# Edge tiles of 125 instead of 128 in a graph network on one core

## The chip, the cores and the metric

One core of one Trainium2 chip runs the whole network as one program. The metric is the device time of one execution in microseconds. The kernel before takes 9366.73 us as the median of 3 runs (9366.05 to 9370.35).

## The reference

A graph of N = 6250 nodes with 128 features has E = 200000 edges, sorted by their target node. There is an attention layer and then three layers of message passing, each of which goes over all edges:

```python
# attention layer
xh = (x @ W).reshape(-1, H, C)                      # H = 4 heads of C = 32
alpha = leaky_relu((xh[dst]*a_i).sum(-1) + (xh[src]*a_j).sum(-1), 0.2)
alpha = softmax of alpha over the edges of each dst
x = layernorm(x + segment_sum(xh[src] * alpha, dst))
# three layers of message passing (h is batch-normalised from the second on)
hk  = relu(concat(h[dst], h[src]) @ linA_w.T + linA_b)
w   = sigmoid(hk @ linB_w.T + linB_b)
prop = segment_sum(w * h[src], dst)
h   = relu(concat(h, prop) @ lin_w.T + lin_b)
# end
x = layernorm(x + h @ final_w.T + final_b)
```

## The kernel before, in words

The edges are cut into groups of GE = 512, that is T = 4 tiles of P = 128 edges. Edge p*4 + t of a group lies on partition p in tile t. 200000 edges make 391 groups and a part of one; the list is filled up to NG = 392 groups with edges whose target lies outside every window. Since the targets are sorted, one group touches few neighbouring nodes: its results go into a window of W = 32 nodes that begins at the group's lowest target (a list of further windows exists for groups that need more).

Each of the four passes over the edges is one pipeline over the groups, and the five engines meet only through semaphores:

- GpSimd fetches the rows of the source nodes, 256 floats or 1 KB for each edge. A group takes four indirect DMAs (line 579), one for each tile, of 128 rows each. They go into one of U = 8 buffers of `G`. A gather waits until the buffer is free and until ACT has copied the group's indices into a small tile `idx`; ACT does this four groups ahead (LOOKAHEAD).
- SP loads for each group the offsets of its targets in the window, broadcast over the partitions (`relbc`, from the table `REL` in DRAM), and 32 rows of the target side (`awin` in message passing, `sm` in attention).
- VectorE makes two one-hot matrices: `sel` (edges on partitions, `make_sel`, line 965) and its transpose `selT16` (window nodes on partitions, `make_selT`, line 969). The latter reads `relbc` in order of p and t, and writes bf16 so that each tile's 128 columns lie together: the source is one run of 512, the target 128 steps of p with 4 of t inside, 256 bytes apart.
- TensorE expands the target side to edges (`selT16` times `awin` or `rhs16`), and sums the weighted rows into the window (`G` times `selw` or `R` times `sel`). VectorE adds the hidden layer (line 1341), takes the logits (line 1352), ACT the sigmoid, and VectorE adds the window to `acc`.

Every engine works through its own steps in an order written out by hand (`mp_order`, `gat_order`), with fixed lags between the stages. In the attention layer there are about 25 VectorE operations for each group, in message passing about a dozen.

Before the first pass SP loads the two lists of edges (lines 413 and 414: 97 rows of 2048 numbers, and the remaining 1344 numbers in a row of their own) and behind them all weights. VectorE turns the lists into window bases and offsets, TensorE transposes them into `rel_all` and `idx_all`, and the table of the attention layer is made and stored. ACT loads x with five DMAs of blocks of 125 rows meanwhile. Between the passes come dense stages over the nodes, in blocks of 125.

Of the kernel before, what the change touches and what calls it, by code (L numbers as in the profile page):

```python
# [15 lines left out]
I32 = mybir.dt.int32  # L16
BF16 = mybir.dt.bfloat16
ALU = mybir.AluOpType
ACT = mybir.ActivationFunctionType

P = 128
T = 4
GE = P * T
# [67 lines left out]
def gnn_kernel(nc, x, src, dst, W0, att, linA_w, linA_b, linB_w, linB_b, lin_w, lin_b, gamma, beta, final_w, final_b,  # L91
# [8 lines left out]
    assert NG % U == 0 and QP <= P and L * 4 * D + D <= U * T * 2 * D - N // NB * D  # L100
    QW = GE * CQ
    QF = E // QW
# [20 lines left out]
    with ExitStack() as ctx:  # L123
# [20 lines left out]
        idx_all = sb("idx_all", [P, (NG + LOOKAHEAD) * T], I32)  # L144
        rel_all = sb("rel_all", [P, NG * T])
        idx = sb("idx", [P, U * T], I32)
# [6 lines left out]
        xrel = sb("xrel", [P, T])  # L153
        xidx = sb("xidx", [P, T], I32)
# [7 lines left out]
        ring = sb("ring", [P, 8, GE])  # L162
        relbc = ring[:, 0:4, :]
        selT = ring[:, 4:8, :]
        pen = sb("pen", [P, 2, GE])
        sel = sb("sel", [P, U, T * W])
        selw = sb("selw", [P, 4, T * W])
        selT16 = selT.bitcast(BF16)[:, :, 0:GE]
        awin = sb("awin", [S * W, 4, D], BF16)
        junk = sb("junk", [P, GE])  # L170
        weighted = sb("weighted", [P, 4, T * D])
        R = weighted[:, 0:2, :]
        ex = weighted[:, 2:4, :]
# [5 lines left out]
        e8 = sb("e8", [P, 2, T, 2 * H])  # L179
        den4 = sb("den4", [H, 2, W])  # L180
        al = sb("al", [P, 2, 4, T * H])
# [4 lines left out]
        logit = sb("logit", [P, 4, T])  # L186
        gate = sb("gate", [P, 4, T])
# [222 lines left out]
        def _(sp):  # L410
            sp.wait_ge(pads_filled, 2)
            for tile, lst in ((dstI, dst), (srcI, src)):
                sp.dma_start(tile[0:QF, :], lst[0:QF * QW].rearrange("(q e) -> q e", e=QW)).then_inc(edges_loaded, 16)
                sp.dma_start(tile[QF:QF + 1, 0:E - QF * QW],  # L414
                             lst[QF * QW:E].rearrange("(q e) -> q e", q=1)).then_inc(edges_loaded, 16)

# [56 lines left out]
            def gat_window(k0, off):  # L473
# [3 lines left out]
                sp.dma_start(relbc[:, off % 4, :], REL[bass.ds(k0 + off, 1), :].rearrange("o e -> (o e)")  # L477
# [9 lines left out]
            with extra_windows(sp, 0) as at:  # L487
                sp.wait_ge(x_free, at.w + (at.q + 1))
                sp.sem_inc(waited, 1)
                sp.dma_start(relbc[:, 0, :], REL[bass.ds(at.g, 1), :].rearrange("o e -> (o e)")  # L490
# [14 lines left out]
            with sp.Fori(0, L) as l:  # L505
# [22 lines left out]
                def window(k0, off):  # L528
# [3 lines left out]
                    sp.dma_start(relbc[0:S * W, off % 4, :], REL[bass.ds(k0 + off, 1), :].rearrange("o e -> (o e)")  # L532
# [11 lines left out]
                with extra_windows(sp, l + 1) as at:  # L544
                    sp.wait_ge(x_free, at.w + (at.q + 1))
                    sp.sem_inc(waited, 1)
                    sp.dma_start(relbc[0:S * W, 0, :], REL[bass.ds(at.g, 1), :].rearrange("o e -> (o e)")
# [15 lines left out]
        def _(pool):  # L563
# [8 lines left out]
            def gather(table, width, k0, off, before, freed):  # L572
# [891 lines left out]
        def _(pe):  # L1464
# [40 lines left out]
            def gat_sjT(k0, off, done=gat):  # L1505
# [4 lines left out]
                for t in range(T):  # L1510
                    i = tr(PS[off % 2][:, P * t:P * t + P], Grows[:, off % U, t, D:2 * D], ident[:, :])  # L1511
# [210 lines left out]
```

## Time and profile before

| | |
|---|---|
| median of 3 runs | 9366.73 us |
| span of the profiled execution | 9351.7 us |
| GpSimd busy | 6739.1 us, 72% |
| VectorE busy | 6023.4 us, 64% |
| TensorE busy | 4974.9 us, 53% |
| ACT busy | 1410.9 us, 15% |

The page gives for the profiled execution its span, from the first to the last instruction, and no total of its own; the median of the runs lies 15 us above that span. The share of an engine counts its instructions from start to end. A gather on GpSimd counts for as long as GpSimd makes the list of transfers for it; the rows themselves arrive later, by the DMA engines. What an engine waits for is inferred from the semaphores; "issue" means that nothing in the profile explains the pause.

### The profile page before, as it was taken

The numbers are of one execution on the slowest core, as the hardware profiler recorded it, in microseconds if no ns is written. First come the engines' busy times: TensorE is split into PE (matmuls) and PEld (weight loads), VectorE is DVE, ScalarE is ACT, GpSimd is POOL, SyncE is SP. The second block draws the span as 40 slices with busy tenths as digits, with TensorE's granted clock in tenths as the row PEclk, the third lists the DMA queues.
The fourth block names the chain that finished last, engine by engine and source line by source line (L and its number), as shares of the span: only waits on it lengthen the run. The fifth ranks groups of instructions, "written<-read, shape, count | busy, mean of one in ns | idle before, by whom it ended". The sixth has DMA issues, their size and how long they took to land.

```text
span 9351.7 us, 148690 instructions
## 1 busy us (share of the span) xinstructions
PE 4974.9 (53%) x27078; PEld 4220.6 (45%) x27079; DVE 6023.4 (64%) x26793; ACT 1410.9 (15%) x5406; POOL 6739.1 (72%) x6331
## 2 busy tenths in 40 slices
PE   2777777777744444444454444444445444444445
PEld 1666666666633333333343333333334333333334
DVE  4888888888856555555556555655555555555656
ACT  1222222222410000000020000000002000000002
POOL 1777777777457777777746777777773777777774
PEclk7555555555555555555565555555556555555555
DMA  2444444444344444444434444444443444444443
GB/s 81 138 137 138 138 138 137 137 138 138 92 137 138 138 138 138 138 138 137 138 109 133 139 138 138 139 138 138 138 135 108 139 137 138 139 138 139 138 139 100
DMA packets 752005, 1241.72 MB, mean 133 GB/s; under 512 B 323315, under 2 KB 387641, under 8 KB 751419
## 3 DMA queue, kind: packets, MB, share of 16 engines
q0 software_dynamic: 301056, 822.48, 30.2%
q1 hardware_dynamic: 444380, 413.53, 15.6%
q10 hardware_dynamic: 6275, 3.20, 0.1%
q14 instruction: 283, 2.32, 0.1%
q8 instruction: 11, 0.18, 0.0%
HBM read 1194.48 MB, written 44.13 MB: 132 GB/s over the span
## 4 chain that ended last, share of the span: by engine, by line
POOL 54%; issue 24%; DMA 6%; DVE 5%; PE 5%; SPq 2%; DVEq 1%; POOLq 1%; ACT 0%; ACTq 0%
POOL G L579 54%; DMA G<-mp_rows,idx 3%; DMA G<-gat_rows,idx 2%; PE ps L1646 2%; DVE junk L1352 1%; SPq L520 1%; PE ps L1551 1%; SPq L513 1%; DMA gat_rows<-ring 1%; DMA mp_rows<-acc 0%; PE ps L1511 0%; DVEq L957 0%; SPq L414 0%; DMA mp_dst_rows<-acc 0%; PE ps L1676 0%
## 5 line engine op out<-in xcount | busy, mean ns | idle before, releaser
L579 POOL DMA_INDIRECT G<-mp_rows,idx x4704 | 4920.1, 1046 | 1810.7 <-issue 1391.1
L1646 PE MATMUL ps<-selw,G 128*128 128x32 f32 x9408 | 2222.2, 400 | 468.8 <-DVE selw L1360 462.9
L1646 PEld LDWEIGHTS ps<-selw,G 128*128 128x128 f32 x9408 | 2093.9, 327 | 751.2 <-issue 652.3
L1341 DVE TENSOR_TENSOR pen<-ps,G 128x512 f32<-128x512 f32 x1176 | 813.1, 691 | 2502.2 <-DMA G<-mp_rows,idx 2500.0
L1636 PE MATMUL ps<-awin,ring 96*128 96x128 bf16 x4704 | 714.5, 307 | 2986.2 <-DVE ring L969 2986.2
L969 DVE TENSOR_SCALAR ring<-ring,pF 96x512 bf16<-96x512 f32 (+1 forms) x1568 | 2178.9, 1390 | 2.5 <-DMA sm<-gat_si 2.1
L579 POOL DMA_INDIRECT G<-gat_rows,idx x1568 | 1779.5, 1135 | 552.7 <-issue 526.5
L1636 PEld LDWEIGHTS ps<-awin,ring 96*128 96x128 bf16 x4704 | 404.2, 130 | 3142.9 <-DVE ring L969 3142.9
L1352 DVE SCALAR_TENSOR_TENSOR junk<-pen,cur 128x128 f32<-128x128 f32 x4704 | 1282.3, 328 | 0.1
L787 ACT ACTIVATE gate<-logit,cur 128x4 f32<-128x4 f32 x1176 | 349.6, 297 | 5870.5 <-DVE junk L1352 5263.8
L1551 PE MATMUL ps<-sel,weighted 128*128 128x32 f32 x3136 | 750.7, 404 | 0.0
L1551 PEld LDWEIGHTS ps<-sel,weighted 128*128 128x128 f32 x3136 | 698.0, 327 | 25.3
L1511 PE MATMUL ps<-ident,G 128*128 128x128 f32 x1568 | 428.7, 429 | 345.3 <-DMA G<-gat_rows,idx 344.9
L666 ACT ACTIVATE pen<-ring,negbig 128x512 f32<-128x512 bf16 x392 | 282.9, 722 | 1518.8 <-DVE ring L969 1518.8
L965 DVE TENSOR_TENSOR sel<-iotaF,rel_all 128x128 f32<-128x128 f32 x1568 | 449.6, 287 | 13.0 <-issue 11.6
L996 DVE CUSTOM_DVE_ANT_0 junk<-ps,pen 128x512 f32<-128x512 f32 x392 | 268.7, 685 | 291.0 <-issue 240.9
L1511 PEld LDWEIGHTS ps<-ident,G 128*128 128x128 f32 x1568 | 280.6, 217 | 363.6 <-issue 236.7
L1352 DVE DVE_READ_ACCUMULATOR junk<-pen,cur 128x1 f32 x4704 | 378.8, 81 | 0.0
L1360 DVE TENSOR_TENSOR selw<-sel,gate 128x128 f32<-128x128 f32 x1176 | 334.6, 285 | 0.2
L654 ACT COPY idx<-idx_all 128x4 int32 (+1 forms) x1572 | 284.3, 182 | 40.7 <-issue 40.6
L1105 DVE TENSOR_TENSOR weighted<-G,weighted 128x512 f32<-128x512 f32 x392 | 270.9, 691 | 0.0
L1523 PE MATMUL ps<-rhs,ring 128*128 128x24 bf16 x1568 | 106.6, 184 | 281.4 <-DVE rhs L1035 281.3
(176 smaller groups left out, 5146.1 us busy)
## 6 DMA issues: line engine op xcount, KB each, us to landing
ring<-rel_dst SPq DMA_DIRECT2D x1176, 192.0 KB
ring<-rel_dst SPq DMA_DIRECT2D x392, 256.0 KB
G<-mp_rows,idx POOLq DMA_INDIRECT x4704
awin<-mp_dst_rows SPq DMA_DIRECT2D x1176, 24.0 KB
G<-gat_rows,idx POOLq DMA_INDIRECT x1568
mp_rows<-acc SPq DMA_DIRECT2D x30, 625.0 KB
mp_dst_rows<-acc SPq DMA_DIRECT2D x30, 468.8 KB
sm<-gat_si SPq DMA_DIRECT2D x392, 0.5 KB
```

The lines of the kernel that those rows point to most:

```text
L579: pool.indirect_dma_start(out=G[:, u, width * t:width * (t + 1)], out_offset=None, in_=table, in_offset=bass.IndirectOffsetOnAxis(ap=idx[: ...
L654: nc.scalar.copy(idx[:, T * (off % U):T * (off % U) + T], idx_all[:, bass.ds(k0 * T + off * T, T)]).then_inc(idx_ready, 1)
L787: nc.scalar.activation(gate[:, off % 4, :], logit[:, off % 4, :], ACT.Sigmoid, bias=cur[:, C_BB:C_BB + 1]).then_inc(done["gate"], 1)
L965: v.tensor_tensor(sel[:, off % U, :].rearrange("p (t n) -> p t n", t=T), iotaW, rel4, ALU.is_equal).then_inc(made, 1)
L969: v.tensor_scalar(tile[0:rows, off % 4, :].rearrange("n (t p) -> n p t", t=T), relbc[0:rows, off % 4, :].rearrange("n (p t) -> n p t", t=T ...
L1341: v.tensor_tensor(pen[:, off % 2, :].rearrange("p (t c) -> p t c", t=T), PS[off % 2][:, :].rearrange("p (t c) -> p t c", t=T), Grows[:, of ...
L1352: v.scalar_tensor_tensor(junk[:, P * t:P * t + P], pen[:, off % 2, P * t:P * t + P], 0.0, cur[:, C_B:C_B + D], ALU.max, ALU.mult, accum_ou ...
L1360: v.tensor_tensor(selw[:, off % 4, :].rearrange("p (t n) -> p t n", t=T), sel[:, off % U, :].rearrange("p (t n) -> p t n", t=T), gate[:, o ...
L1511: i = tr(PS[off % 2][:, P * t:P * t + P], Grows[:, off % U, t, D:2 * D], ident[:, :])
L1551: i = mm(PS[4 + b][:, 0:W], R[:, b, D * t:D * t + D], sel[:, off % U, W * t:W * t + W], start=(t == 0), stop=(t == T - 1))
L1636: i = mm(PS[off % 2][:, D * t:D * t + D], selT16[0:S * W, off % 4, P * t:P * t + P], awin[:, off % 4, :], start=True, stop=True)
L1646: i = mm(PS[2 + off % 2][:, 0:W], Grows[:, off % U, t, 0:D], selw[:, off % 4, W * t:W * t + W], start=(t == 0), stop=(t == T - 1))
```

## The change

A tile has EP = 125 edges, so a group has GE = 500, and 200000 edges are exactly NG = 400 groups on QP = 100 rows of 2000 numbers. No edge is filled in. All tensors with edges on partitions have 125 of them; each gather has 125 rows; `selT16` keeps its buffer but uses 500 of its columns, 125 for each tile. Each list is loaded with one DMA. Everything else stays: the window of 32, the 8 buffers, the orders and lags.

```diff
-GE = P * T
+EP = 125
+GE = EP * T
...
-    QF = E // QW
...
-        idx = sb("idx", [P, U * T], I32)
+        idx = sb("idx", [EP, U * T], I32)
...
-        ring = sb("ring", [P, 8, GE])
+        ring = sb("ring", [P, 8, P * T])
+        Gedge = Grows[0:EP]
...
             for tile, lst in ((dstI, dst), (srcI, src)):
-                sp.dma_start(tile[0:QF, :], lst[0:QF * QW].rearrange("(q e) -> q e", e=QW)).then_inc(edges_loaded, 16)
-                sp.dma_start(tile[QF:QF + 1, 0:E - QF * QW],
-                             lst[QF * QW:E].rearrange("(q e) -> q e", q=1)).then_inc(edges_loaded, 16)
+                sp.dma_start(tile, lst.rearrange("(q e) -> q e", e=QW)).then_inc(edges_loaded, 16)
...
                     pool.indirect_dma_start(
-                        out=G[:, u, width * t:width * (t + 1)], out_offset=None, in_=table,
+                        out=G[0:EP, u, width * t:width * (t + 1)], out_offset=None, in_=table,
                         in_offset=bass.IndirectOffsetOnAxis(ap=idx[:, T * u + t:T * u + t + 1], axis=0),
                     ).then_inc(gathered[u], 16)
...
             def make_selT(k0, off, tile, rows, node, made):
                 v.tensor_scalar(tile[0:rows, off % 4, :].rearrange("n (t p) -> n p t", t=T),
-                                relbc[0:rows, off % 4, :].rearrange("n (p t) -> n p t", t=T),
+                                relbc[0:rows, off % 4, 0:GE].rearrange("n (p t) -> n p t", t=T),
                                 node, None, ALU.is_equal).then_inc(made, 1)
...
-                        i = mm(PS[off % 2][:, D * t:D * t + D], selT16[0:S * W, off % 4, P * t:P * t + P],
+                        i = mm(PS[off % 2][0:EP, D * t:D * t + D], selT16[0:S * W, off % 4, EP * t:EP * t + EP],
                                awin[:, off % 4, :], start=True, stop=True)
```

## Rows read from the trace of the kernel before

**Rows 1.** The page: span, and busy time of each engine (share of the span).
```profile
span 9351.7 us, 148690 instructions
PE 4974.9 (53%) x27078; PEld 4220.6 (45%) x27079; DVE 6023.4 (64%) x26793; ACT 1410.9 (15%) x5406; POOL 6739.1 (72%) x6331
```

**Rows 2.** The chain that ended last: shares by engine; SPq is SP's queue.
```profile
POOL 54%; issue 24%; DMA 6%; DVE 5%; PE 5%; SPq 2%; DVEq 1%; POOLq 1%; ACT 0%; ACTq 0%
```

**Rows 3.** Line 579, GpSimd's gathers: duration min/median/max; idle before them.
```profile
L579 POOL DMA_INDIRECT G<-mp_rows,idx x4704: 942/947/1943, 2605.0 to 9267.3; - x196
L579 POOL DMA_INDIRECT G<-gat_rows,idx x1568: 942/948/1979, 196.5 to 2452.5; - x196
  issue: 1917.7, 6048
  ACT idx L654: 154.8, 155
```

**Rows 4.** The page's groups for the gathers: busy us, mean ns of one.
```profile
L579 POOL DMA_INDIRECT G<-mp_rows,idx x4704 | 4920.1, 1046 | 1810.7 <-issue 1391.1
L579 POOL DMA_INDIRECT G<-gat_rows,idx x1568 | 1779.5, 1135 | 552.7 <-issue 526.5
```

**Rows 5.** Waits: who waited for whom; us in total, times, longest.
```profile
DVE pen L1341 <- DMA G<-mp_rows,idx: 2500.0, 1143, 3.9
```

**Rows 6.** Timelines, GpSimd and VectorE: start us, duration us, what.
```profile
4000.87 1.36 DVE L969 TENSOR_SCALAR ring<-ring,pF 96x512 bf16<-96x512 f32 x1
4001.09 1.45 POOL L579 DMA_INDIRECT G<-mp_rows,idx  x1 [0.30 <-issue]
4002.84 0.95 POOL L579 DMA_INDIRECT G<-mp_rows,idx  x1 [0.30 <-issue]
...
1205.57 1.72 POOL L579 DMA_INDIRECT G<-gat_rows,idx  x1 [0.30 <-issue]
1205.79 1.38 DVE L969 TENSOR_SCALAR ring<-ring,pF 128x512 bf16<-128x512 f32 x1
```

**Rows 7.** Line 969 on VectorE: duration min/median/max in ns.
```profile
L969 DVE TENSOR_SCALAR ring<-ring,pF x1568: 1347/1357/1604, 203.7 to 9265.5; 96x512 bf16<-96x512 f32 x147, 128x512 bf16<-128x512 f32 x49
```

**Rows 8.** Two windows: us, then busy us (instructions) of PE, PEld, DVE, ACT, POOL.
```profile
300.00:2300.00 2000.00, 1469.68 (x10077) 1256.50 (x10078) 1629.59 (x8707) 582.86 (x1740) 1577.37 (x1388) 0.50 0.49 138
2700.00:4500.00 1800.00, 832.86 (x4002) 708.57 (x4002) 1071.71 (x4332) 131.27 (x666) 1394.80 (x1331) 0.50 0.48 138
```

**Rows 9.** VectorE operations that show its pace: duration, or group mean.
```profile
L879 DVE CAST acc<-acc x1: 1227/1227/1227, 76.5 to 76.5; 98x2048 f32<-98x2048 int32 x1
L881 DVE TENSOR_REDUCE moreF<-acc x1: 2286/2286/2286, 77.7 to 77.7; 98x4 f32<-98x2048 f32 x1
L1299 DVE TENSOR_SCALAR ring<-mh x150: 210/221/440, 2573.0 to 7148.4; 128x125 f32 x90, 128x125 f32<-128x125 f32 x60
L893 DVE COPY rel_all<-ps x4: 818/826/843, 90.5 to 93.1; 128x392 f32<-128x392 f32 x4
L929 DVE TENSOR_SCALAR ring<-ps 125x128 f32<-125x128 f32 x50 | 14.5, 291 | 33.3 <-DMA gat_rows<-ring 31.3 <-PE ps L1500 1.8
```

**Rows 10.** The start: SP's issue of a list, and the two waits.
```profile
5.62 11.05 SPq L414 DMA_DIRECT2D acc<-in_dst  x1
17.38 30.66 SPq L414 DMA_DIRECT2D acc<-in_src  x1
DVE acc L879 <- DMA acc<-in_src: 66.4, 1, 66.4
PE ps L1468 <- DMA params<-in_L_gnn_lin_b: 86.6, 1, 86.6
```

**Rows 11.** DMA queues (packets, MB, share of 16 engines); one issue.
```profile
q0 software_dynamic: 301056, 822.48, 30.2%
q10 hardware_dynamic: 6275, 3.20, 0.1%
G<-in_x ACTq DMA_DIRECT2D x5, 625.0 KB
```

More of the change, by code:

```diff
@@ L99, in gnn_kernel @@
     NG = QP * CQ
-    assert NG % U == 0 and QP <= P and L * 4 * D + D <= U * T * 2 * D - N // NB * D
     QW = GE * CQ
-    QF = E // QW
+    assert NG % U == 0 and QP <= P and QW * QP == E and L * 4 * D + D <= U * T * 2 * D - N // NB * D
     NT = N // (NB * BU)
@@ L142, in gnn_kernel @@
         relF = mh[0:QP, 0:QW]
-        idx_all = sb("idx_all", [P, (NG + LOOKAHEAD) * T], I32)
-        rel_all = sb("rel_all", [P, NG * T])
-        idx = sb("idx", [P, U * T], I32)
+        idx_all = sb("idx_all", [EP, (NG + LOOKAHEAD) * T], I32)
+        rel_all = sb("rel_all", [EP, NG * T])
+        idx = sb("idx", [EP, U * T], I32)
         per_group = sb("per_group", [P, NG], I32)
@@ L152, in gnn_kernel @@
         shift = sb("shift", [P, 1])
-        xrel = sb("xrel", [P, T])
-        xidx = sb("xidx", [P, T], I32)
+        xrel = sb("xrel", [EP, T])
+        xidx = sb("xidx", [EP, T], I32)
         baseF = sb("baseF", [P, CQ])
@@ L161, in gnn_kernel @@
         Grows = G[:, :, :].rearrange("p u (t c) -> p u t c", t=T)
-        ring = sb("ring", [P, 8, GE])
+        ring = sb("ring", [P, 8, P * T])
+        Gedge = Grows[0:EP]
         relbc = ring[:, 0:4, :]
         selT = ring[:, 4:8, :]
-        pen = sb("pen", [P, 2, GE])
-        sel = sb("sel", [P, U, T * W])
-        selw = sb("selw", [P, 4, T * W])
+        pen = sb("pen", [P, 2, P * T])
+        sel = sb("sel", [EP, U, T * W])
+        selw = sb("selw", [EP, 4, T * W])
         selT16 = selT.bitcast(BF16)[:, :, 0:GE]
         awin = sb("awin", [S * W, 4, D], BF16)
-        junk = sb("junk", [P, GE])
+        junk = sb("junk", [P, P * T])
         weighted = sb("weighted", [P, 4, T * D])
-        R = weighted[:, 0:2, :]
-        ex = weighted[:, 2:4, :]
+        R = weighted[0:EP, 0:2, :]
+        ex = weighted[0:EP, 2:4, :]
         mx = sb("mx", [P, 4, 2])
@@ L178, in gnn_kernel @@
         dg = sb("dg", [P, 2, S, W], BF16)
-        e8 = sb("e8", [P, 2, T, 2 * H])
+        e8 = sb("e8", [EP, 2, T, 2 * H])
         den4 = sb("den4", [H, 2, W])
-        al = sb("al", [P, 2, 4, T * H])
+        al = sb("al", [EP, 2, 4, T * H])
         mnew = sb("mnew", [P, 2, W])
@@ L185, in gnn_kernel @@
         tt = sb("tt", [P, 2, 2, 2 * W])
-        logit = sb("logit", [P, 4, T])
-        gate = sb("gate", [P, 4, T])
+        logit = sb("logit", [EP, 4, T])
+        gate = sb("gate", [EP, 4, T])
         flat = ring[:, :, :].rearrange("p a b -> p (a b)")
@@ L588, in gather_extra @@
                     pool.indirect_dma_start(
-                        out=G[:, 0, TW * t:TW * (t + 1)], out_offset=None, in_=table,
+                        out=G[0:EP, 0, TW * t:TW * (t + 1)], out_offset=None, in_=table,
                         in_offset=bass.IndirectOffsetOnAxis(ap=xidx[:, t:t + 1], axis=0)).then_inc(x_rows, 16)
@@ L665, in gat_pen @@
                 act.wait_ge(done["selT"], k0 + (off + 1))
-                nc.scalar.activation(pen[:, off % 2, :], selT16[:, off % 4, :], ACT.Identity, bias=negbig[:, 0:1],
+                nc.scalar.activation(pen[:, off % 2, 0:GE], selT16[:, off % 4, :], ACT.Identity, bias=negbig[:, 0:1],
                                      scale=BIG).then_inc(done["pen"], 1)
@@ L876, in _ @@
             assert done[0] == PREP_CONST
-            dve.wait_ge(edges_loaded, 64)
+            dve.wait_ge(edges_loaded, 32)
             then(v.tensor_copy(dstF, dstI))
@@ L1162, in make_extra_sel @@
                 v.tensor_scalar(tile[0:rows, 0, :].rearrange("n (t p) -> n p t", t=T),
-                                relbc[0:rows, 0, :].rearrange("n (p t) -> n p t", t=T),
+                                relbc[0:rows, 0, 0:GE].rearrange("n (p t) -> n p t", t=T),
                                 shift[0:rows, 0:1], node, ALU.subtract, ALU.is_equal).then_inc(selT_done, 1)
```

50 lines of the change are left out of this document (25 added, 25 removed).

## The prediction

> **What bounds the kernel now.** I read the busy times first, then the chain of waits, then the groups of the gather line, and last short timelines. The busy times [rows 1] put GpSimd first at 72% of the span, and the chain [rows 2] names its gathers for 54% and "issue" for 24%. The reader is to see in the gather line [rows 3] that nearly all idle time before a gather has nobody behind it: 1917.7 us over 6048 gathers is 0.30 us each, while ACT's index copies account for 154.8 us. So GpSimd issues one gather, pauses 0.30 us, issues the next, and the others follow: VectorE stands 2500.0 us in the message passing waiting for rows [rows 5]. An undisturbed gather takes 0.947 us. Four of them with their pauses are 4 x (0.947 + 0.30) = 4.99 us a group. That is the floor of a group. The actual group is longer: in the two windows [rows 8] there are 1388/4 = 347 groups in 2000 us (5.76 us each, attention layer) and 1331/4 = 333 groups in 1800 us (5.41 us each, message passing).
>
> Where is the rest? The mean gather is 1046 and 1135 ns [rows 4], against medians of 947 and 948 ns [rows 3]. The excess is 4920.1 - 4704 x 0.947 = 465 us and 1779.5 - 1568 x 0.948 = 293 us, together **758 us**. The timelines [rows 6] say what it is. The gather that starts at 4001.09 lasts 1.45 us and the next one 0.95; VectorE's L969 (the transposed one-hot, 512 elements) runs from 4000.87 to 4002.23, and the gather ends 0.31 us behind it. In the attention layer the gather at 1205.57 lasts 1.72 us, L969 ends at 1207.17 and the gather 0.12 us later. A gather cannot finish while L969 runs. L969 is 1.357 us long by its median [rows 7] and there is one in each group.
>
> **The change part by part.** (a) *More groups.* 392 become 400 in each of four passes, so 6400 gathers for 6272: 128 x 1.247 = 160 us more, if a gather of 125 rows costs what one of 128 does. Bounds for a gather: in proportion to rows 0.925 us (-142 us over 6400); the other end is the first rival. I take 0.947, because no row shows a smaller one and the start and end of an instruction do not shrink with rows.
>
> (b) *L969.* Its source is one run of 512 values, its target 128 rows of 4 (p outside, t inside). Afterwards: one run of 500, and 125 rows of 4. What makes it stop GpSimd? Copies in SBUF run two elements at a time here: the cast of 2048 values takes 1227 ns and the reduction of as many 2286 ns [rows 9]. I read this as the instruction taking a second path to memory, splitting its data in halves, and GpSimd needing that same path. Line 1299, 125 elements of SBUF on both sides, takes 221 ns by its median; line 929, the same kind of operation on 128 elements out of PSUM, 291 ns [rows 9]. The 70 ns between them are what 125 elements cost less at 0.60 in place of 1.12 ns each (65 ns). So an odd count is no obstacle when both sides have it. With 500 on one side and 125 on the other the halves no longer correspond: 500 halves at 250, which is row 62 and a half of 125. I expect it to fall back to one element at a time on one path, and GpSimd not to be stopped. By the Trainium skill, page "VectorE: DVE Perf Modes", section "Mode 2×_2P", this mode needs an outermost non-unit dimension that is even, or odd and equal on both sides; 500 against 125 is neither. The page "SBUF — State Buffer", section "Who interferes with whom", has the same mode and GpSimd exclude one another; by that, the trace agrees, with ends 0.12 and 0.31 us behind L969.
>
> Of the 758 us I take 90%, 680 us, as removed; the rest I leave to short casts and to operations with two inputs in SBUF, which stay.
>
> How long L969 then is, no row shows. Low end: 500 elements at the reduction's pace of 2286/2048 = 1.12 ns, 0.56 us. High end: now 256 steps of two in 1.357 us; 500 steps of equal length are 2.65 us. Nearest is line 893 [rows 9], which writes single elements with gaps: 392 in 826 ns, 2.1 ns each, so 1.05 us. I take 1.05 to 1.36, no longer than now. Its cover: VectorE is busy 1629.59/347 = 4.70 us a group in the attention layer and 1071.71/333 = 3.22 us in the message passing [rows 8], under 4.99 in both. At 2.65 us it would be 5.99 and 4.51: the attention layer would go over.
>
> (c) *Loading the edge list.* Each list was loaded as 97 rows of 8 KB and a rest. SP stands 30.66 us in issuing the second [rows 10], before it 11.05 us for the first; all weights queue behind, TensorE waits 86.6 us for the last of them and VectorE 66.40 us for the list, and that is on the chain of the start. Now it is one load of 100 rows each. A load of 125-row blocks by ACT is 6250 packets of rows and 25 more, 5 for each of 5 DMAs [rows 11]: five engines share it, five being what divides 125 and is at most 16. 97 is prime, so one engine does all 97; 100 would go on ten. The 42 us of issue fall to a few: **-40 us**, with bounds of 0 and -43, once.
>
> (d) *Everything else* (125 partitions in place of 128, 500 in place of 512 columns in ACT's and VectorE's instructions, the two memsets and the transposes of 125 columns) is on engines that wait for GpSimd. At most 12/512 of an instruction. I set 0. Without the cover, in the attention layer, VectorE's slack is 4.99 - 4.70 = 0.29 us a group, and its loads would still fit. The lists of indices are copied four groups ahead, some 20 us, so that a gather landing a microsecond later delays only the end of a pass.
>
> Sum against the profiled execution: 9351.7 - 680 + 160 - 40 = 8792 us of span. The median of the runs is 9366.7, 15 us above the span. So 8807, rounded **8810 us**, 5.9% below before.
>
> **Rivals.** *First, the other side: 125 rows go on five engines, and building the list for them is slower.* [Rows 11] show it for the ACT queue. The gathers now make 301056/6272 = 48 packets, 3 for each of 16 engines, so 8 rows per engine; five engines would have 25 rows each. If GpSimd writes for all engines side by side, the part that writes grows by 25/8. That part is what a gather still does once L969 lets go, 0.12 to 0.31 us: +0.25 to +0.66 us a gather, times 6400 = +1600 to +4200 us, giving 10410 to 13000 us. It decides from +0.087 us a gather (557/6400). For it: the packets of ACT's loads, and the shape of GpSimd's work as the stall shows it. Against: GpSimd's DMAs need not be shared out as ACT's are, and the engine's work may be per row. The skill's page "DMA: Bandwidth & Descriptors", section "Why a DMA increments its semaphore by 16 and not by 1", says that the largest number up to 16 that divides both row counts is taken, and grants the software-generated direct copies an exception. It speaks against this change. With it alone and a flat price per gather the sum would stay 8810, since consecutive gathers start on different engines.
>
> *Second: L969 stays in the two-path mode.* Then (b) gives nothing and 32 more groups bring 32 x 758/1568 = 15 us of stall: 9367 + 160 + 15 - 40 = 9500 us. For it: L969 takes 1.357 us, hardly a two-at-a-time speed, so that its mode is read only from whom it stops.
>
> *Third: L969 doubles (2.65 us).* Message passing is unharmed, attention becomes VectorE's at 5.99 us: 8810 + 400 x 1.0 = 9210 us.
>
> *Fourth: the gather gets cheaper with its rows*, 8810 - 142 = 8670, or a little under.
>
> **How the numbers follow.** Forecast 0.50, first rival 0.28, second 0.10, third 0.08, fourth 0.04. The forecast's own range is 8700 to 8950. The whole range must go from the fourth case to the lower end of the first rival: 8640 to 10400 leaves out some 0.03 below and half of the first rival above, 0.14. A change under 0.2% could not be told from none here. Faster: 0.50 + 0.08 + 0.04 less 0.02 = 0.60; slower 0.37; the same 0.03, mostly a first rival that costs just what the stalls give.
>
> **What would show it.** In the profile after: gathers with mean near median, 0.95 to 0.97 us, also where L969 lies beside them (b); a group of 5.0 to 5.1 us in both windows; 6400 gathers; the wait for `in_src` and TensorE's first wait some 40 us shorter, and the first gather before 160 us in place of 196.5 (c). A median gather above 1.03 us makes the forecast wrong, and then the packets per gather (48 now) say whether five engines carry it. Stalls as now beside L969 mean the second rival; VectorE without idle time in the attention layer the third.

## The result and the profile after

The changed kernel takes 10731.9 us as the median of 4 runs (10726.06 to 10734.05), beside 9368.54 us (9366.05 to 9372.19, 4 runs) for the kernel before: a ratio of 1.1455, interval 1.1439 to 1.1471. It is 14.6% slower. The forecast was 8810 us, with a range up to 10400. In one set of the runs below, e1 to e3, which ran on another chip than the later ones (15, they on 4), the kernel before took 10917.72 us (10876.9 to 10972.25, 7 runs) in place of some 9363, for a reason that no trace here shows; ratios of that set are beside that number, and what rests on them was run again.

The page of the kernel after: the span, the busy time of each engine, then the chain that ended last.

```profile
span 10732.3 us, 151490 instructions
PE 5282.3 (49%) x27598; PEld 4610.9 (43%) x27599; DVE 7883.0 (73%) x27305; ACT 1423.2 (13%) x5494; POOL 7887.8 (73%) x6459
...
POOL 48%; issue 28%; DVE 10%; PE 5%; DMA 4%; DVEq 2%; SPq 2%; POOLq 1%; ACT 0%; ACTq 0%
```

Two engines have grown against [rows 1]: GpSimd by 1149 us and VectorE by 1860 us. The chain has the same two leaders as in [rows 2], and VectorE at twice its share. Which instructions grew is in the views by line. Below are the gathers (now line 578) and the transposed one-hot (now line 968): duration min/median/max in ns, first and last start.

```profile
L578 POOL DMA_INDIRECT G<-mp_rows,idx x4800: 1207/1214/1558, 3007.9 to 10647.7; - x192
L578 POOL DMA_INDIRECT G<-gat_rows,idx x1600: 1207/1214/1728, 142.3 to 2839.0; - x178
...
L968 DVE TENSOR_SCALAR ring<-ring,pF x1600: 2408/2414/2431, 150.1 to 10646.6; 96x500 bf16<-96x500 f32 x133, 128x500 bf16<-128x500 f32 x45
```

Beside [rows 3] and [rows 7], the shortest gather went from 942 to 1207 ns and the median from 947 to 1214: a gather is 0.267 us longer. Line 968 went from 1357 to 2414 ns. The longest message passing gather fell from 1943 to 1558 ns, and the page's means show the same:

```profile
L578 POOL DMA_INDIRECT G<-mp_rows,idx x4800 | 5875.7, 1224 | 1832.9 <-issue 1711.9
L578 POOL DMA_INDIRECT G<-gat_rows,idx x1600 | 1972.6, 1233 | 802.1 <-issue 506.1
```

Mean over median is 10 and 19 ns here, where [rows 3, 4] have 99 and 187. A timeline of GpSimd and of VectorE says why (start, duration, what):

```profile
4000.35 1.21 POOL L578 DMA_INDIRECT G<-mp_rows,idx  x1 [0.30 <-issue]
4001.86 1.21 POOL L578 DMA_INDIRECT G<-mp_rows,idx  x1 [0.30 <-issue]
...
3999.40 2.41 DVE L968 TENSOR_SCALAR ring<-ring,pF 96x500 bf16<-96x500 f32 x1
...
4004.61 0.69 DVE L1340 TENSOR_TENSOR pen<-ps,G 125x512 f32<-125x512 f32 x1 [1.58 <-DMA G<-mp_rows,idx]
```

The gather at 4000.35 starts and ends (4001.56) inside line 968, which runs to 4001.81, and takes its usual 1.21 us. In [rows 6] both gathers beside that line ended only behind it. The queue of the gathers (packets, MB, share of 16 engines) has changed too:

```profile
q0 software_dynamic: 819200, 826.65, 30.3%
```

That is 819200/6400 = 128 packets for each gather, against 48 in [rows 11], for fewer rows. The records of the packets in the trace have their sizes: of the data, 30 packets of 4096 bytes (4 rows) and 5 of 1024 bytes (1 row) for each gather, where the kernel before has 32 of 4096. Five engines with 25 rows each make just that, 5 x (6 x 4 + 1) rows; sixteen engines with 8 rows each, the last with 5, would make 31 and 1. What the other packets are, the run of sizes below shows.

Where the time went, by windows (us, then busy us and instructions of PE, PEld, DVE, ACT, POOL, then granted clock, busy share of the DMA engines and GB/s), one in the attention layer and one in message passing:

```profile
300.00:2200.00 1900.00, 1258.17 (x8072) 1089.04 (x8071) 1618.41 (x6968) 459.22 (x1395) 1381.23 (x1121) 0.50 0.46 114
3400.00:4400.00 1000.00, 420.94 (x1960) 372.46 (x1961) 703.33 (x2130) 64.60 (x328) 800.66 (x655) 0.50 0.48 120
```

With four gathers a group these are 280 and 164 groups: **6.78** us a group in attention and **6.11** in message passing, where [rows 8] give 5.76 and 5.41. In message passing 4 x (1.222 + 0.305) = 6.11: GpSimd alone sets it. In attention that floor would be 6.15 and the group is 0.6 us above it. Over the passes: 400 x 6.78 - 392 x 5.76 = +454 us, 1200 x 6.11 - 1176 x 5.41 = +970 us, and the first gather starts at 142.3 us in place of 196.5 [rows 3], -54 us. The sum is +1370 of the 1380.6 us by which the span grew.

### The profile page after: what moved, and what is told of

Read it like the earlier page. It is cut to its first block, busy times and chain, and to the rows that moved or that the text cites. A ratio compares the mean times of both kernels' runs of the same rounds, so it can differ in the third digit from the quotient of the medians.

```text
span 10732.3 us, 151490 instructions
## 1 busy us (share of the span) xinstructions
PE 5282.3 (49%) x27598; PEld 4610.9 (43%) x27599; DVE 7883.0 (73%) x27305; ACT 1423.2 (13%) x5494; POOL 7887.8 (73%) x6459
## 3 DMA queue, kind: packets, MB, share of 16 engines
q0 software_dynamic: 819200, 826.65, 30.3%
## 4 chain that ended last, share of the span: by engine, by line
POOL 48%; issue 28%; DVE 10%; PE 5%; DMA 4%; DVEq 2%; SPq 2%; POOLq 1%; ACT 0%; ACTq 0%
POOL G L578 48%; DMA G<-mp_rows,idx 3%; PE ps L1522 2%; DVE sm L1006 1%; DVE junk L1351 1%; SPq L512 1%; DVE sel L964 1%; SPq L519 1%; DVE rhs L1034 1%; PE ps L1550 1%; DVEq L956 1%; DMA gat_rows<-ring 1%; DVE weighted L1104 0%; DVE sm L1012 0%; DVE mh L1097 0%
## 5 line engine op out<-in xcount | busy, mean ns | idle before, releaser
L578 POOL DMA_INDIRECT G<-mp_rows,idx x4800 | 5875.7, 1224 | 1832.9 <-issue 1711.9
L968 DVE TENSOR_SCALAR ring<-ring,pF 96x500 bf16<-96x500 f32 (+1 forms) x1600 | 3863.2, 2415 | 2.5 <-DMA sm<-gat_si 2.1
L1635 PE MATMUL ps<-awin,ring 96*125 96x128 bf16 x4800 | 826.2, 327 | 3821.8 <-DVE ring L968 3821.8
L1645 PE MATMUL ps<-selw,G 125*128 125x32 f32 x9600 | 2267.6, 400 | 448.3 <-DVE selw L1359 448.3
L1645 PEld LDWEIGHTS ps<-selw,G 125*128 125x128 f32 x9600 | 2136.7, 328 | 642.1 <-issue 560.3
L1340 DVE TENSOR_TENSOR pen<-ps,G 125x512 f32<-125x512 f32 x1200 | 829.5, 691 | 2104.8 <-DMA G<-mp_rows,idx 2102.9
L1635 PEld LDWEIGHTS ps<-awin,ring 96*125 96x125 bf16 x4800 | 601.4, 218 | 3984.1 <-DVE ring L968 3984.1
L1351 DVE SCALAR_TENSOR_TENSOR junk<-pen,cur 125x128 f32<-125x128 f32 x4800 | 1375.5, 339 | 0.1
L1550 PE MATMUL ps<-sel,weighted 125*128 125x32 f32 x3200 | 766.1, 404 | 0.0
L1550 PEld LDWEIGHTS ps<-sel,weighted 125*128 125x128 f32 x3200 | 712.2, 327 | 25.8
```

The lines of the kernel that those rows point to most:

```text
L578: pool.indirect_dma_start(out=G[0:EP, u, width * t:width * (t + 1)], out_offset=None, in_=table, in_offset=bass.IndirectOffsetOnAxis(ap=id ...
L968: v.tensor_scalar(tile[0:rows, off % 4, :].rearrange("n (t p) -> n p t", t=T), relbc[0:rows, off % 4, 0:GE].rearrange("n (p t) -> n p t", ...
L1340: v.tensor_tensor(pen[0:EP, off % 2, :].rearrange("p (t c) -> p t c", t=T), PS[off % 2][0:EP, :].rearrange("p (t c) -> p t c", t=T), Gedge ...
L1351: v.scalar_tensor_tensor(junk[0:EP, P * t:P * t + P], pen[0:EP, off % 2, P * t:P * t + P], 0.0, cur[0:EP, C_B:C_B + D], ALU.max, ALU.mult, ...
L1550: i = mm(PS[4 + b][:, 0:W], R[:, b, D * t:D * t + D], sel[:, off % U, W * t:W * t + W], start=(t == 0), stop=(t == T - 1))
L1635: i = mm(PS[off % 2][0:EP, D * t:D * t + D], selT16[0:S * W, off % 4, EP * t:EP * t + EP], awin[:, off % 4, :], start=True, stop=True)
```

## The experiments

Three causes stand to be told apart, all of them in the prediction: the 125-row gather is dearer because five engines carry it (first rival); line 968 has lost the two-path mode, which frees GpSimd (the forecast) but doubles the line (third rival); the edge lists load faster. Each can be done or undone alone. Kernels of one set ran on one chip beside the kernel before.

**The kernel after again (e5).** Nothing was changed.

> The kernel after, unchanged, beside the kernel before in the same stretch of chip time. In the last group of runs the kernel before took 10918 us instead of 9369 with the same program, and gathers whose list took 0.949 us were waited for longer. Theory C (that stretch had slower landings of rows, which a kernel of 16-engine gathers at 1.25 us each feels and one of 1.5 us each hardly does): where the kernel before is again near 10900, the kernel after is near 10750 to 10950, that is no slower; where the kernel before is near 9370, the kernel after is 10730. Rival D (everything is slower by a factor): the ratio stays at 1.145.

Measured: 10712.89 us (10708.24 to 10721.68), ratio 1.1443 (1.1424 to 1.1462) beside 9363.19 us. The result repeats, and the numbers below are held against this one.

**Only the 125-row gather, put into the kernel before (e8).** The groups stay 512 edges in tiles of 128; from the ninth group of each pass a gather fetches 125 rows, so that the last three edges of a tile work on old rows. The same edit from the first group on (e4) gives no time, since those edges then have no rows at all.

```diff
+                def rows(n, t):
+                    return dict(out=G[0:n, u, width * t:width * (t + 1)], out_offset=None, in_=table,
+                                in_offset=bass.IndirectOffsetOnAxis(ap=idx[0:n, T * u + t:T * u + t + 1], axis=0))
+                if isinstance(k0, int):
+                    for t in range(T):
+                        pool.indirect_dma_start(**rows(P, t)).then_inc(gathered[u], 16)
+                else:
+                    for t in range(T):
+                        pool.indirect_dma_start(**rows(125, t)).then_inc(gathered[u], 16)
```

> The kernel before, with only the gathers changed to 125 rows after the first eight groups of each pass; the last three edges of a tile keep older rows, so part of the work is left out. L969 with both paths stays. Theory A: undisturbed gathers 1.214 us, 128 packets each; message passing 6.1 to 6.5 us a group and attention 6.1 to 6.8 us, 9367 + about 1500 us = 10700 to 11100 us where the kernel before is near 9370. Rival B (the shape of the gather costs nothing, groups of 500 do): the time of the kernel before.

Measured: 10641.56 us (10639.77 to 10650.6), ratio 1.1366 (1.1347 to 1.1385). Its gathers and the one-hot, then the two windows (the same columns as above):

```profile
L586 POOL DMA_INDIRECT G<-mp_rows,idx x4608: 1180/1201/2202, 2978.1 to 10554.7; - x192
L583 POOL DMA_INDIRECT G<-mp_rows,idx x96 | 92.5, 964 | 299.0 <-DMA mp_rows<-acc 270.6
...
300.00:2200.00 1900.00, 1228.20 (x8427) 1053.89 (x8427) 1410.17 (x7259) 505.05 (x1452) 1545.86 (x1163) 0.50 0.46 120
3400.00:4400.00 1000.00, 400.07 (x1924) 340.43 (x1924) 524.40 (x2080) 63.12 (x320) 804.94 (x641) 0.50 0.45 118
```

Line 583 has the gathers of 128 rows in the same execution, 964 ns in the mean and 949 by the median; line 586 those of 125, 1201 ns by the median. Three rows fewer cost 0.25 us more. The windows have 1900/(1163/4) = 6.53 us a group in attention and 1000/(641/4) = 6.24 in message passing. This one edit makes 1278 us of slowdown, nearly as much as the whole change (the expectation's lowest time was 10700). The stalls are still there (up to 2202 ns), since the one-hot was left alone.

**Only the gathers taken back to 128 rows in the kernel after (e1, e9).** Tiles stay 125 edges; three rows that nobody reads are fetched with each. The index tiles get 128 partitions and are zeroed once.

```diff
-        idx_all = sb("idx_all", [EP, (NG + LOOKAHEAD) * T], I32)
+        idx_all = sb("idx_all", [P, (NG + LOOKAHEAD) * T], I32)
...
-        idx = sb("idx", [EP, U * T], I32)
+        idx = sb("idx", [P, U * T], I32)
...
-                        out=G[0:EP, u, width * t:width * (t + 1)], ...
+                        out=G[:, u, width * t:width * (t + 1)], ...
```

> The kernel after, with each gather of 128 rows instead of 125: the three extra partitions of every tile fetch row 0 and nobody reads them. Groups stay at 500 edges, so L968 stays as it is. Theory A (a gather costs what its most loaded engine has rows: 25 now, 8 then): the gather falls from 1.214 to 0.947 us, a message-passing group from 6.08 to about 5.0 us, the three passes by 3 x 400 x 1.07 = 1280 us; the attention pass, which waits for VectorE, stays near 6.7 us a group or loses up to 0.3. Time 9350 to 9450 us. Theory B (the price lies in the groups of 500, in the longer L968 or in the DMA traffic, not in the shape of the gather): gathers stay near 1.2 us and the time above 10500.

Measured in the first set (e1): 11363.97 us, ratio 1.0406 (1.0365 to 1.0447), beside an expected 9350 to 9450. The gather's median is 0.949 us, as expected, but the time says little: VectorE waited 2024.9 us before line 1343, which adds the rows of message passing, and the profile names nothing on this core for it. So it was run again.

> The same kernel as e1 (after, with gathers of 128 rows of which three are unread; L968 unchanged, 2.41 us on one path), hoped for beside a kernel before near 9363 us. Gathers 0.947 us. Theory A: the message passing is bound by GpSimd again, 4.99 to 5.1 us a group instead of 6.1, so 3 x 400 x 1.05 = 1260 us less than the kernel after; the attention pass is bound by VectorE and its exchange with TensorE and stays at 6.5 to 6.7 us a group. Time 9400 to 9450 us. Rival (VectorE with 2.41 us binds message passing as well once gathers are short): 9700 us or more. Beside a slow kernel before (near 10900) it is near 11360 again.

Measured (e9): 9429.16 us (9423.8 to 9430.03), ratio 1.0071 (1.0055 to 1.0086) beside 9361.9 us. Its gathers, the one-hot, its queue and the windows:

```profile
L579 POOL DMA_INDIRECT G<-mp_rows,idx x4800: 941/949/1064, 2918.9 to 9338.3; - x192
L579 POOL DMA_INDIRECT G<-mp_rows,idx x4800 | 4635.3, 966 | 1852.5 <-issue 1447.2
L579 POOL DMA_INDIRECT G<-gat_rows,idx x1600 | 1535.5, 960 | 1145.4 <-ACT idx L654 591.4
L971 DVE TENSOR_SCALAR ring<-ring,pF x1600: 2407/2414/2436, 152.7 to 9336.7; 96x500 bf16<-96x500 f32 x133, 128x500 bf16<-128x500 f32 x45
...
q0 software_dynamic: 307200, 839.27, 30.9%
...
300.00:2200.00 1900.00, 1302.70 (x8359) 1127.78 (x8358) 1660.84 (x7203) 474.09 (x1440) 1107.87 (x1155) 0.50 0.44 119
3400.00:4400.00 1000.00, 507.99 (x2364) 449.70 (x2364) 842.66 (x2562) 77.80 (x394) 760.21 (x787) 0.50 0.53 146
```

307200/6400 is 48 packets again, and 1284 us are gone. This is the forecast's kernel with its assumption about the gather made true, so its windows test the rest. Message passing: 787/4 = 197 groups, **5.08** us each, as forecast (5.0 to 5.1). Attention: 1155/4 = 289 groups, **6.58** us, where the forecast had about 5.05. GpSimd is busy 58% of that window and VectorE 87%: there VectorE sets the pace, and e7 below shows that it is the one-hot.

**A one-hot without the two-path mode, in the kernel before (e3, e10).** The same elements in the same order, but as an operation on two tensors, the node number broadcast as the second one.

```diff
-                v.tensor_scalar(tile[0:rows, off % 4, :].rearrange("n (t p) -> n p t", t=T),
+                v.tensor_tensor(tile[0:rows, off % 4, :].rearrange("n (t p) -> n p t", t=T),
                                 relbc[0:rows, off % 4, :].rearrange("n (p t) -> n p t", t=T),
-                                node, None, ALU.is_equal).then_inc(made, 1)
+                                node.unsqueeze(2).to_broadcast([rows, P, T]), ALU.is_equal).then_inc(made, 1)
```

> The kernel before, with L969 as a comparison of two tensors (the node numbers broadcast as second tensor) in the same order of elements, so that it cannot use both paths; 128 rows and 512 edges stay. Theory A (one element at a time, each step as long as a step of two before): L969 takes 512/500 x 2.41 = 2.47 us and stops no gather: message passing 4 x 1.25 = 5.0 us a group instead of 5.41 (-480 us), attention 6.6 to 6.7 us a group instead of 5.76 (+350 us): about 9240 us. Rival (the longer L968 in the kernel after came from the odd pitch of 125, not from the lost path): L969 stays near 1.36 us or shorter and the time is about 8700 us.

> The same kernel as e3: the kernel before with L969 as a comparison of two tensors in the old order. It showed 2.42 us for L969, twice as long, and gathers of 1.30 us in the mean that were stopped all the same (longest 2.7 us), so a second tensor read from SBUF stops GpSimd too. Expected beside a kernel before near 9363: message passing 4 x (1.30 + 0.31) = 6.4 us a group, attention 6.7 to 7.0: about 11000 us. Rival (the length came from the slow stretch of that job): L969 1.36 us and no change of time.

Measured: in the first set (e3) 11510.68 us, ratio 1.0539 (1.0504 to 1.0573); run again (e10) 10827.92 us (10820.53 to 10830.5), ratio 1.1562 (1.1544 to 1.1579). The gathers and the one-hot of e10, and a piece of its timeline:

```profile
L579 POOL DMA_INDIRECT G<-mp_rows,idx x4704: 942/946/2712, 2860.9 to 10742.9; - x196
L969 DVE TENSOR_TENSOR ring<-ring,pF x1568: 2417/2421/2493, 204.3 to 10741.6; 96x512 bf16<-96x512 f32 x147, 128x512 bf16<-128x512 f32 x49
...
4003.60 0.95 POOL L579 DMA_INDIRECT G<-mp_rows,idx  x1 [0.31 <-issue]
4004.85 2.17 POOL L579 DMA_INDIRECT G<-mp_rows,idx  x1 [0.30 <-issue]
...
4004.27 2.42 DVE L969 TENSOR_TENSOR ring<-ring,pF 96x512 bf16<-96x512 f32 x1
```

The length is the same as in the kernel after, 2421 for 2414 ns: one element at a time, each step 4.7 to 4.8 ns. But the gather beside it is held, from 4004.85 to 4007.02, and ends 0.33 us behind line 969 (4006.69). An operation with two inputs in SBUF stops GpSimd as well, for nearly twice as long as the two-path one did, and e3's expectation that no gather would be held is false. So e10 shows the length of a single-path step, not what freeing GpSimd brings. The Trainium skill, page "SBUF — State Buffer", section "Who interferes with whom", says both that an operation with two SBUF inputs contends with GpSimd's reads and, as an inference, that descriptor generation is not held by it; here the gather is held, with a longest of 2712 ns against a median of 946. A gather also reads its row numbers from `idx` in SBUF, so the first statement may be enough for this; the run doesn't tell the two apart.

**A one-hot that is one plain run (e2, e6, e7).** Edge t*128 + p of a group goes to partition p of tile t (t*125 + p in the kernel after). Then source and target of the one-hot are both one run, with no hops.

```diff
-                v.tensor_scalar(tile[0:rows, off % 4, :].rearrange("n (t p) -> n p t", t=T),
-                                relbc[0:rows, off % 4, :].rearrange("n (p t) -> n p t", t=T),
+                v.tensor_scalar(tile[0:rows, off % 4, :],
+                                relbc[0:rows, off % 4, :],
                                 node, None, ALU.is_equal).then_inc(made, 1)
...
-                               lst[:, GE * c:GE * c + GE].rearrange("q (p t) -> q p t", t=T)[:, :, t],
+                               lst[:, GE * c:GE * c + GE].rearrange("q (t p) -> q p t", t=T)[:, :, t],
```

On the kernel after with its 125-row gathers (e2), in the first set:

> The kernel after, with edge t*125 + p of a group in tile t instead of edge p*4 + t, so that L968 reads and writes one run of 500 on both sides. Gathers stay at 125 rows. Theory A (VectorE's long L968 binds only the attention pass; the message passing is bound by gathers of 1.214 us): L968 falls from 2.41 to about 0.42 us, the attention group from 6.74 to about 6.1 us, message passing stays at 6.1: 10732 - 400 x 0.65 = about 10470 us. Since 500 on both sides splits evenly, the instruction stops GpSimd again, but only for 0.4 us. Rival (L968 costs in all four passes): below 10000 us.

Measured: 10546.56 us, ratio 0.9657 (0.9624 to 0.969). Line 968 has a median of 472 ns, the gathers one of 1211. GpSimd's longer gathers set its pace: both passes stay near 4 x (1.23 to 1.27 + 0.305) us a group. Since the kernel after was not run in that set, this run doesn't say what the plain run is worth to it. On the kernel before (e6), and on the kernel after with 128-row gathers (e7):

> The kernel before with edge t*128 + p in tile t, so that L969 is one run of 512 on both sides, 128 rows for each gather. Theory A (GpSimd's stalls are the length of L969 with both paths): L969 0.42 to 0.53 us, GpSimd stopped at most half as often and long, message passing 5.0 to 5.15 us a group and attention 5.0 to 5.2: where the kernel before takes 9370, about 8800 us. Rival (the stalls have another cause and only coincide with L969): no change. Where rows land slowly (the kernel before near 10900) the gain may be smaller.

> The kernel after with both costs removed: gathers of 128 rows (three of them unread) and L968 as one run of 500. Theory A (the 400 groups by themselves cost only 2% more gathers): e6 plus 128 x 1.25 us = 160 us, less 54 us for the shorter start, about 1.012 times e6. Rival (groups of 500 or tiles of 125 have a cost of their own on TensorE or VectorE): more than 1.03 times e6.

Measured, beside 9363.19 us: e6 8854.34 us (8848.54 to 8865.79), ratio 0.9458 (0.9442 to 0.9473); e7 8869.33 us (8868.43 to 8875.11), ratio 0.9471 (0.9455 to 0.9486). The one-hot and the gathers of e6, then the attention window of e7:

```profile
L969 DVE TENSOR_SCALAR ring<-ring,pF x1568: 470/477/731, 206.6 to 8763.8; 96x512 bf16<-96x512 f32 x147, 128x512 bf16<-128x512 f32 x49
L579 POOL DMA_INDIRECT G<-mp_rows,idx x4704: 942/946/1407, 2391.9 to 8764.3; - x196
...
300.00:2200.00 1900.00, 1593.10 (x10447) 1396.71 (x10447) 1455.02 (x9006) 600.56 (x1803) 1460.83 (x1442) 0.50 0.56 149
```

512 elements take 477 ns instead of 1357, 0.93 ns each against the 1.12 of an operation that goes one at a time [rows 9], so still in the two-path mode, and gathers are still held (the longest takes 1407 ns), but for a third as long at most. e7 against e9 isolates the form of the one-hot in the kernel with tiles of 125: its line has a median of 471 ns, 9429 - 8869 = 560 us are gone, and the attention window goes from 6.58 to 1900/(1442/4) = 5.27 us a group. e7 had been put some 1.2% above e6 for its 128 additional gathers; it is 0.2% above. The earlier lists were in that sum already (first gather at 143.7 instead of 198.9 us); what was not is that its gathers are held less: above 0.947 or 0.946 us each, the gathers lose 187 us in e7 and 268 in e6. Why they are held less, no run shows.

**Gathers of other sizes (e11).** In the kernel before, from the ninth group on, odd groups gather 128, 120, 126 and 124 rows, even ones 112, 64, 100 and 127. Rows not fetched are left out of the work.

```diff
+                    if off % 2:
+                        pool.indirect_dma_start(**rows(128, 0)).then_inc(gathered[u], 16)
+                        pool.indirect_dma_start(**rows(120, 1)).then_inc(gathered[u], 16)
+                        pool.indirect_dma_start(**rows(126, 2)).then_inc(gathered[u], 16)
+                        pool.indirect_dma_start(**rows(124, 3)).then_inc(gathered[u], 16)
...
```

> The kernel before with gathers of different sizes after the first eight groups of each pass, each on a line of its own (part of the work is left out): 128, 120, 126 and 124 rows in the odd groups, 112, 64, 100 and 127 in the even ones. Theory A (length = 0.82 us + 15.7 ns for each row of the most loaded engine, where the number of engines is the largest up to 16 that divides the rows; from 8 rows in 0.947 us and 25 in 1.214): 128 0.95, 120 (15 engines, 8 rows) 0.95, 126 (14, 9) 0.96, 124 (4, 31) 1.31, 112 (7 rows) 0.93, 64 (4) 0.88, 100 (10 engines, 10 rows) 0.98, 127 (1 engine, 127) 2.8 us. Rival (only full 16 have a fast path, everything else the price of 125): 120, 126, 100 near 1.2 us as well.

Measured once (10899.9 us): lines 586 to 589 are 128, 120, 126 and 124 rows, 591 to 594 are 112, 64, 100 and 127.

```profile
L586 POOL DMA_INDIRECT G<-mp_rows,idx x576: 1132/1205/1648, 3007.3 to 10807.2; - x192
L587 POOL DMA_INDIRECT G<-mp_rows,idx x576: 986/993/1100, 3008.8 to 10808.7; - x192
L588 POOL DMA_INDIRECT G<-mp_rows,idx x576: 995/999/1371, 3010.1 to 10810.0; - x192
L589 POOL DMA_INDIRECT G<-mp_rows,idx x576: 1292/1297/1309, 3011.7 to 10811.3; - x192
L591 POOL DMA_INDIRECT G<-mp_rows,idx x576: 940/944/1433, 2999.5 to 10799.7; - x192
L592 POOL DMA_INDIRECT G<-mp_rows,idx x576: 912/916/942, 3001.3 to 10801.0; - x192
L593 POOL DMA_INDIRECT G<-mp_rows,idx x576: 1002/1007/1989, 3002.5 to 10802.2; - x192
L594 POOL DMA_INDIRECT G<-mp_rows,idx x576: 2565/2982/3581, 3004.5 to 10804.3; - x192
```

Take the number of engines as the largest divisor of the rows up to 16, and look at the rows that each then has. 64: 4 rows, 916 ns. 112: 7 rows, 944. 128: 8 rows, 947 (in its own kernel). 120 on 15: 8 rows, 993. 126 on 14: 9 rows, 999. 100 on 10: 10 rows, 1007. 125 on 5: 25 rows, 1214 (in the kernel after). 124 on 4: 31 rows, 1297. 127 on 1: 127 rows, 2565 at the least. The duration goes with this number and not with the rows: 124 rows cost more than 125, and 127 far more than either. Between 8 and 25 rows an engine's row costs 15.7 ns, from 31 to 127 about 13 ns by the least duration.

The packets settle it. Past the first eight groups each size is gathered 768 times. By this rule, with up to 4 rows in a packet, the eight sizes together make 201 packets of 4096 bytes, 21 of 3072, 10 of 2048 and 14 of 1024; the trace has 154368, 16128, 7680 and 10752, which is 768 times these numbers. All other packets are of 4, 8, 12 and 16 bytes, and their numbers (99840, 4608, 20736 and 435456) are 768 times what comes out when each gather ends with one of 4 bytes on all 16 engines and an engine that carries no row gets 4 bytes in place of each row that a carrying engine has. In the kernel after that makes 16 x 8 = 128 packets a gather. So GpSimd's list has 16 entries for each row of an engine, 16 x 25 = 400 for 125 rows and 16 x 8 = 128 for 128 rows. The trace doesn't name the engine of a packet; that the idle ones get these fillers follows from the numbers, which agree for every size. That only counts divisible by 16 are cheap, the rival in that expectation, is false: 120, 126 and 100 cost 40 to 60 ns over 128, no more. A 128-row gather right behind the 127-row one takes 1205 ns; why was not pursued, and the order of the sizes was not varied, so a part of the 40 to 60 ns can come from what stands before them.

**The version that beats both (e12).** The kernel before with the plain-run one-hot of e6, and with its lists loaded as 96 rows, one row and the rest.

```diff
-                sp.dma_start(tile[0:QF, :], lst[0:QF * QW].rearrange("(q e) -> q e", e=QW)).then_inc(edges_loaded, 16)
+                sp.dma_start(tile[0:QF - 1, :],
+                             lst[0:(QF - 1) * QW].rearrange("(q e) -> q e", e=QW)).then_inc(edges_loaded, 16)
+                sp.dma_start(tile[QF - 1:QF, :],
+                             lst[(QF - 1) * QW:QF * QW].rearrange("(q e) -> q e", q=1)).then_inc(edges_loaded, 16)
```

> e6 (before, L969 as one run of 512) with each list of edges loaded as 96 rows, one row and the rest instead of 97 rows and the rest. Theory A (96 rows go over 16 engines, 97 over one): the weights come 40 us earlier, the first gather at about 145 us instead of 199, and the time is 40 to 54 us below e6: about 8805 us where the kernel before takes 9363. Rival (the start is bound by the loads of x and the table): below e6 by less than 10 us.

Measured: 8812.0 us (8799.69 to 8815.53, 5 runs), ratio 0.9407 (0.9394 to 0.9419), 42 us below e6. Its first gather starts at 139.7 us, 59 us before that of e6. SP's issues of the first list and the start of the second (start, duration):

```profile
5.22 0.40 SPq L413 DMA_DIRECT2D acc<-in_dst  x1
5.68 0.31 SPq L415 DMA_DIRECT2D acc<-in_dst  x1
6.04 0.23 SPq L417 DMA_DIRECT2D acc<-in_dst  x1
6.31 0.33 SPq L413 DMA_DIRECT2D acc<-in_src  x1
```

The rows of the kernel before [rows 10] need care: line 414, where SP stood 11.05 and 30.66 us, is the list's last, single row of 1344 numbers, not the load of 97 rows, which line 413 issued in 0.35 and 0.62 us. In e12 the same single row (line 417) is issued in 0.23 us. So it isn't dear by itself; SP stands at the next issue behind a load of 97 rows, and behind one of 96 it doesn't.

## Why the prediction was wrong

**Step (a), more groups: this failed.** It priced a gather of 125 rows at 0.947 us, "because no row shows a smaller one", though its bounds ran up to the first rival. Measured is 1.214 us, because five engines carry 25 rows each and the list grows with the rows of one engine. Over 6400 gathers that is 6400 x 0.267 = 1709 us of GpSimd's time; the time itself moves by 1278 us (e8) or 1284 us (e9 against e5), since a part falls where GpSimd was held or was not the bound: in attention e9 has 6.58 us a group and the kernel after only 6.78. The first rival had the mechanism (five engines), the place of decision (+0.087 us a gather) and a price of +0.25 to +0.66 us that holds the measured 0.267 at its low end (its premise that GpSimd writes for all engines side by side is what the packets show; the 0.12 us at which it put the part that grows was read from a single gather), and its lowest time, 10410, is 3% under what came. It got 0.28 and should have been the forecast. (200000 edges of 512 a group are 390 groups and a part of one, not the 391 of the description; the sums go by the 392 that are gathered, and stay.)

Its grounds against were weak. The prediction had the packets of ACT's 125-row loads [rows 11] and the 48 packets of a gather, 3 for each of 16 engines, which is what the same rule gives for 128. The Trainium skill, page "DMA: Bandwidth & Descriptors", section "Why a DMA increments its semaphore by 16 and not by 1", excepts some software-generated direct copies; a gather is indirect, and its packets follow the rule. With the rule and the flat price the prediction would have kept 8810; what the forecast left out, and its rival had, was that GpSimd's list grows with the rows of one engine.

**Step (b), line 969 leaves the two-path mode: right, and GpSimd is no longer stopped.** In e9 the means are 966 and 960 ns with medians of 949 and 947 (forecast 0.95 to 0.97 us), and message passing has its 5.08 us a group. By that half 680 us were to go; the 758 us over the medians in the kernel before are 4635.3 - 4800 x 0.949 = 80 us and 1535.5 - 1600 x 0.947 = 20 us in e9, so 658 us of stall went. That the unequal odd count is what ends the mode is the prediction's reading; no run varies the count. The prediction's pause of 0.30 us between gathers was rounded down (1917.7/6048 is 0.317), which leaves its 4.99 us a group a little under the 5.08.

**The length of that line failed too.** It was set at 1.05 to 1.36 us, "no longer than now"; it is 2.414 us. The nearest row taken, line 893, is a different operation out of PSUM. The working had the right answer as its high end: 500 steps of the present length, 2.65 us. A two-path step took 1357/256 = 5.3 ns, a single-path step 2414/500 = 4.8 ns, so losing the mode nearly doubles the line. The third rival (0.08) said exactly this, with attention at 5.99 us a group and 9210 us. Measured in e9: 6.58 and 9429. What it missed is a pause. Below are VectorE's wait at line 998 of e9 (us in total, times, longest) and three starts of that line, which runs once in each group:

```profile
DVE junk L998 <- issue: 256.8, 50, 5.5
...
301.96 0.68 DVE L998 CUSTOM_DVE_ANT_0 junk<-ps,pen 128x500 f32<-128x500 f32 x1 [5.29 <-issue]
...
307.59 0.67 DVE L998 CUSTOM_DVE_ANT_0 junk<-ps,pen 128x500 f32<-128x500 f32 x1
...
313.52 0.67 DVE L998 CUSTOM_DVE_ANT_0 junk<-ps,pen 128x500 f32<-128x500 f32 x1
```

A group without a pause is 313.52 - 307.59 = 5.93 us, the rival's 5.99. But 50 times in 400 groups, once in each turn of the loop of eight, VectorE pauses for 5.1 us (256.8/50); an eighth of that is 0.64 us a group, and 5.93 + 0.64 = 6.57 against 6.58 in the window. The kernel before has the pause as well (240.9 us in 44 pauses before line 996), but there GpSimd has only its 0.30 us between two gathers, (2000 - 1577.37)/1388 [rows 8], so GpSimd sets the pace and the pause is covered; once VectorE sets it, the pause counts. The profile names nobody for it, and no run changed it. The kernel has one thing at that place that the profile doesn't count as busy: at the start of each turn `load_bases` loads 16 window bases into VectorE's registers. That this is the pause is likely and not shown. Message passing was unharmed, as the rival said.

So the failure has two parts. With the gather at its old price the change would have cost 0.7% (e9) and not gained 5.9%; the dearer gather adds 13.7 points (e5 against e9). The forecast treated the rivals as alternatives. Two of them came true together, beside the forecast's own gain.

**Step (c), the lists: right,** though the issue that stands is the one behind the load of 97 rows (e12). -40 us was forecast, -54 us came in the first gather, and e12 shows 42 us for the load alone. VectorE's wait for the lists fell from 66.4 to 9.8 us and TensorE's for the weights from 86.6 to 30.4. SP's issues in the kernel after:

```profile
5.11 0.40 SPq L414 DMA_DIRECT2D acc<-in_dst  x1
5.57 0.32 SPq L414 DMA_DIRECT2D acc<-in_src  x1
```

**Step (d), everything else at nothing: right as far as it shows.** e7 against e6 has all of it, with the 128 gathers, the lists and the gathers held less, at 15 us together. One part of it was not foreseen, the weight loads below.

What stays open: how much a plain-run one-hot would give the kernel after beside a kernel before at 9363 us (its attention floor of 4 x (1.233 + 0.305) = 6.15 us against 6.78 would make some 250 us, an estimate), what VectorE's pause is, and why e7 holds its gathers less than e6.

## What to carry to other kernels

Before a tile loses three of 128 rows, look at what the divisors of the new number do to each transfer: the rows that one DMA engine gets, not the rows in all, set what a gather costs GpSimd. Where a kernel depends on VectorE's two-path mode, ask both what it stops and what its steps cost; a write that hops costs nearly the same per step in either mode (4.8 and 5.3 ns here), and a layout with source and target in one run was worth 5.4% here by itself. And when several rivals rest on independent facts, price them together too.

## What the runs showed of the hardware

- A gather of 125 rows of 1 KB takes GpSimd 1.214 us and makes 128 packets; one of 128 rows takes 0.947 us and makes 48. Engines without rows get as many entries as those with rows, 4 bytes each (by the packet sizes of e11).
- One engine for 127 rows: 2565 ns at the least, and the next gather of 128 rows 1205 instead of 947 ns.
- Writing bf16 in hops of 250 or 256 bytes: 4.8 ns a step with one path, 5.3 ns for two elements with two; in one run 0.93 ns an element (477/512).
- An operation with two inputs in SBUF holds a gather to its end and 0.33 us beyond (e10), although at 2421 ns for 512 elements it goes one at a time.
- SP's next issue behind a load of 97 rows of 8 KB stood 11.05 and 30.66 us; behind 96 or 100 rows the issues take 0.3 to 0.4 us.
- Loading 125 columns of bf16 weights takes longer than loading 128. Groups of the kernel after and, for line 1636, of the kernel before (busy, mean ns):

```profile
L1635 PEld LDWEIGHTS ps<-awin,ring 96*125 96x125 bf16 x4800 | 601.4, 218 | 3984.1 <-DVE ring L968 3984.1
```

```profile
L1636 PEld LDWEIGHTS ps<-awin,ring 96*128 96x128 bf16 x4704 | 404.2, 130 | 3142.9 <-DVE ring L969 3142.9
```

218 against 130 ns. In message passing it lies in TensorE's idle time; what it costs in attention no run isolates.
